# Issuing the last scan of each group behind the first in-projection half of the next group

## What is computed

```
proj = hidden_states @ in_proj_w.T
gate, xBC, dt = split(proj)                      # 8192 gate, 10240 xBC, 128 dt
xBC = silu(causal_conv4(xBC) + conv_b)
x, Bm, Cm = split(xBC)                           # 8 groups of B and C, 128 heads of 64
scores = (C B^T) * exp(segment sums of dt*A)     # per head, causal
Y = scores @ (x*dt) + x*D
yg = Y * silu(gate)
out = yg * rsqrt(mean over the group of yg^2 + eps) * norm_w @ out_proj_w.T
```

## Time and profile before

| | |
|---|---|
| median of 3 runs | 2484.99 us (2480.08 to 2488.39) |
| the profiled execution | 2485.11 us |
| its span, first to last instruction | 2483.3 us |
| mean granted TensorE clock | 0.954 of full |
| PE busy | 2285.2 us, 92% of the span |
| DVE busy | 1697.0 us, 68% |
| ACT busy | 1379.5 us, 56% |
| POOL busy | 846.0 us, 34% |

### The profile page before, as it was taken

The page is one execution under the profiler, slowest core; times in us unless marked ns, Lnnn a source line. Parts: engine busy times, 40 slices in busy tenths (PEclk is TensorE's granted clock), DMA queues, the critical chain, the costliest instruction groups (busy, mean ns, idle before and its releaser), DMA issues. The chain is left out here.

```text
span 2483.3 us, 38330 instructions
## 1 busy us (share of the span) xinstructions
PE 2285.2 (92%) x11624; PEld 1633.1 (66%) x11624; DVE 1697.0 (68%) x2949; ACT 1379.5 (56%) x3105; POOL 846.0 (34%) x681
## 2 busy tenths in 40 slices
PE   6898888897899999999999999999999999987998
PEld 4554545445677776777767777677776777756877
DVE  3555555554797598489579759848957975965345
ACT  4453535403785487388468558737846855852330
POOL 4251423310244244244325414414432541441230
PEclk9699998899999999999999999999999999988999
DMA  5000000001210110111011011011101101002100
GB/s 226 10 1 9 1 1 1 1 0 47 72 34 20 52 31 28 44 31 35 11 60 35 20 52 31 28 48 31 31 24 48 35 20 52 27 1 85 42 18 34
DMA packets 38226, 85.39 MB, mean 34 GB/s; under 512 B 3584, under 2 KB 5888, under 8 KB 37376
## 3 DMA queue, kind: packets, MB, share of 16 engines
q1 hardware_dynamic: 38016, 82.82, 10.1%
HBM read 79.92 MB, written 2.88 MB: 33 GB/s over the span
## 5 line engine op out<-in xcount | busy, mean ns | idle before, releaser
L1643 PE MATMUL b_ps<-xh_keep,wh 128*128 128x512 f32 x1152 | 490.9, 426 | 5.2 <-DVE bc L1398 3.0
L1645 PE MATMUL b_ps<-xh_keep,wl 128*128 128x512 f32 x1152 | 463.1, 402 | 0.0
L1644 PE MATMUL b_ps<-xl_keep,wh 128*128 128x512 f32 x1152 | 463.0, 402 | 0.0
L1434 DVE TENSOR_TENSOR decayed<-decay,b_scores 128x768 f32<-128x768 f32 x256 | 397.8, 1554 | 25.1 <-ACT decay L1162 24.1
L1323 POOL TENSOR_TENSOR wl<-wraw,wh 128x512 fp32r<-128x512 f32 x144 | 190.9, 1326 | 574.7 <-ACT wh L1111 574.7
L1156 ACT ACTIVATE decay<-b_ps,cs 128x256 f32<-128x256 f32 (+1 forms) x1024 | 345.1, 424 | 7.7 <-PE b_ps L1653 7.1
L1398 DVE SCALAR_TENSOR_TENSOR xs<-b_ps,par,xs 128x510 f32<-128x510 f32 (+2 forms) x384 | 284.9, 742 | 93.2 <-ACT xs L1130 80.9
L1643 PEld LDWEIGHTS b_ps<-xh_keep,wh 128*128 128x128 f32 x1152 | 222.0, 193 | 84.2 <-issue 41.5
L1645 PEld LDWEIGHTS b_ps<-xh_keep,wl 128*128 128x128 f32 x1152 | 221.5, 192 | 53.4
L1644 PEld LDWEIGHTS b_ps<-xl_keep,wh 128*128 128x128 f32 x1152 | 223.1, 194 | 42.2
L1524 DVE SCALAR_TENSOR_TENSOR yl<-yg,par,yh 128x512 fp32r<-128x512 f32 x128 | 96.4, 758 | 203.5 <-ACT yh L1177 202.4
(11 more groups left out here) (229 smaller groups left out, 4116.3 us busy)
## 6 DMA issues: line engine op xcount, KB each, us to landing
wraw<-win_dram SPq DMA_DIRECT2D x144, 256.0 KB, 2.6
oraw<-wout_dram SPq DMA_DIRECT2D x8, 2048.0 KB, 9.4
w<-w_dram SPq DMA_DIRECT2D x2, 3584.0 KB, 23.9
fraw<-wgu_dram SPq DMA_DIRECT2D x11, 512.0 KB, 3.5
draw<-wd_dram SPq DMA_DIRECT2D x1, 2816.0 KB, 11.9
xT<-xT_dram SPq DMA_DIRECT2D x4, 512.0 KB, 3.8
x_keep<-x_dram SPq DMA_DIRECT2D x1, 2048.0 KB, 11.2
out_dram<-x_keep SPq DMA_DIRECT2D x8, 256.0 KB, 2.0
```

What stands on the lines that cost most here:

```text
L1434: nc.vector.tensor_tensor(sd[:, b % 2, :, :], ex[:, b % 2, :, :], sm[:, b, :].unsqueeze(1).to_broadcast([P, 2, 3 * P]), ALU.mult)\
L1643: nc.tensor.matmul(out, w_h, x_h, start=(k == 0), stop=False)
L1644: nc.tensor.matmul(out, w_h, x_l, start=False, stop=False)
L1645: last = nc.tensor.matmul(out, w_l, x_h, start=False, stop=(k == KT - 1))
```

## The change

The last scan of a group is no longer issued at the end of `steps`, unless it is the last group. In the loop it is issued after X0_0 of the next group, the first of the four in-projection halves, and ahead of X0_1. Only the order on PE changes. No instruction is added or removed, and the orders of DVE, ACT, POOL and SP stay as they were.

```
@@ in steps(ph, g, last) of the tensor block
                         turn(ph, j + 1, 0)
                         turn(ph, j + 1, 1)
-                scan(ph, UNITS - 1, BATCH - 1)
+                if last:
+                    scan(ph, UNITS - 1, BATCH - 1)
@@ in the loop of the tensor block
                 steps(ph, i, False)
                 for q, c in enumerate(conv_halves(0)):
                     in_half(ph, i, SUBS + 2 + q // 2, c[0])
+                    if q == 0:
+                        scan(ph, UNITS - 1, BATCH - 1)
                 project(ph, i)
                 head_end(ph)
```

## The result

The change made the kernel slower by a third of a percent. The changed kernel takes 2492.72 us (median of 12 runs, 2487.62 to 2498.21), the kernel before 2485.71 us (12 runs, 2480.0 to 2488.39). The ratio is 1.0033, with a 95% interval of 1.0023 to 1.0043. The profiled execution of the changed kernel has a span of 2490.5 us against 2483.3 us, 7.2 us more.

The account below looks back on a forecast made before the run. A chain on DVE, ACT and POOL was taken to bound the stretch from last scan to projection, PE only fitting in. 15.8 us paid, less 1.6 and 1.3, gave +12.8 on 2485.1: 2497.9 us, range 2484 to 2505.

Parts of the forecast that it names:

- PE's wait goes, 19.4 us: Ahead of the last scan in seven loop rounds, PE's wait for DVE's decay product disappears: 7 x 2.77 = 19.4 us.
- The chain holds, and the wait comes back in two parts: DVE, ACT and POOL keep the projection's start at 15.87 us; PE's 2.78 us return as waits of about 2.9 and 2.5.
- Gain in rounds 1 and 7, 1.3 us: From last scan to projection, X0_0 issued sooner brings 16.52 and 16.56 us down to 15.87, 1.3 us gained.
- The clock, 15.8 us paid less 1.6 us: Projection's first two units start at low clock: 7 x 2.25 = 15.8 us paid, less 1.6 that round 3 pays already.
- the two units: Sign: the projection's first two units take 13.3 to 14.6 us, at a granted clock of 0.77 to 0.88.
- Nothing else moves: Elsewhere no change: SP's queue and the DMAs hang on untouched work, and group 7 keeps its order.
- Chain bound, clock kept: Rival at the projection: waits move but the clock rarely falls there; 2483.8 to 2490.6 us; chance 0.20.
- PE bound: Rival: the chain gives way when PE runs ahead, removed wait gained in full, 19.4 us, 2465.7 us; chance 0.07.
- The wait stays: Rival ahead of the last scan: product later than X0_0's end, or X0_0 waits; within 1 us of 2485.1; chance 0.05.
- The wait of line 1734: Sign at the transposes of the sums of squares (line 1733 before): waits for DVE's convolution, 7 x 2.9 = 20 us.
- that of yl: Sign at line 1744 of before: PE's waits for DVE's yl grow from 12.5 us in total to some 24.

## Why the prediction was right, and where it was not

It forecast slower, 2497.9 us in a range of 2484 to 2505; measured were 2492.7 us, or +7.0 us where +12.8 were forecast. The bound of 0.3% that it set for slower was just passed: the ratio is 1.0033, with part of its interval below. That the kernel is slower at all is clear, that it is so by more than 0.3% is not.

*PE's wait goes, 19.4 us.* Right: line 1665 keeps 2.3 us, in group 7.

*The chain holds, and the wait comes back in two parts.* Right. Forecast were 15.87 us, waits of about 2.9 and 2.5 us and PE done 12.15 us after its start; measured 15.88 to 15.89 us from the decay product (15.93 in round 2 before, as 15.87 was counted from the scan), 2.97 and 1.86 to 2.29 us, and 12.3 us in round 2. In four rounds the second wait is 2.29 us, 0.2 less than forecast: the second four transposes begin 12.97 us after the product, not 12.8, and take 0.63 us, not 0.5. In rounds 1, 4 and 7 they take 1.06, 0.77 and 0.76 us, since the low clock has reached them, and the wait is shorter by that. The kernel with matmuls ahead of its scan shows it in all seven rounds, and the one with the scan behind all halves shows where the chain passes.

*Gain in rounds 1 and 7, 1.3 us.* Right; all rounds together gained 1.4 to 1.6.

*The clock, 15.8 us paid less 1.6 us.* Right in mechanism and size. Forecast were +14.2 us for the projection's first two units, measured +14.3 and +14.1. The price per round was 1.9 to 2.9 us above the 11.72 us of the kernel before, with a mean of 2.29; 2.25 was taken. That the two are so near is in part luck: 2.25 was the middle between two ends and not worked out, and the prediction's own mean stretch gave 2.0. The rate behind it held: the low clock covers 34.1 us of these units in the seven rounds, 4.9 us each, and 4.9 x 1.61 / 3.5 is 2.2. It is the clock and not the scan: with the waits filled the two units are at 11.7 us. The Trainium skill, "TensorE: Matmul & The Clock Gate", section "HAM oscillation — how this bites in real kernels", says of a kernel with waits for DMA that the burst of matmuls behind each wait begins cold. The trace of the changed kernel agrees at the projection in all seven rounds (0.79 to 0.85); in the trace of before one wait of 2.8 us in seven left the clock full.

*Nothing else moves.* This is the step that failed, by 5.2 us in the profile, which is most of what lies between +12.8 and +7.2. Two stretches that the change does not touch became shorter, the one ahead of the decay products by 1.4 us and group 7 with what follows by 3.8 us. In group 7 from its first wait in unit 0, to the same place in its last unit (windows, before and then changed):

```profile
2083.86:2201.90 118.04, 115.88 (x648) 82.81 (x649) 105.63 (x124) 96.72 (x206) 49.23 (x35) 0.97 0.07 21
```

```profile
2094.83:2209.97 115.14, 112.99 (x648) 80.99 (x649) 105.39 (x124) 96.49 (x206) 49.22 (x35) 1.00 0.07 22
```

The same matmuls, 2.9 us less: the clock fell in unit 0 of group 7 before and not in the changed kernel. The last 0.9 us of the 3.8 lie behind group 7's last decay product (275.0 us before, 274.1 changed), and no run shows why. Unit 0 of every group has waits of 1.6 and 1.4 us for ACT, behind which the clock falls in some rounds and not in others. Which ones is the same in both profiles of each kernel; my reading is that it hangs on when the waits come, and so on everything ahead of them, which no run isolates. The prediction had priced those low stretches at the same in both kernels. They made 4.3 us of the error: 2.9 in group 7, and 1.4 in the rounds, where both kernels have 30.6 us of them but in different places. The kernel with these waits filled shows what they are worth in all: 16.5 us.

*Rivals.* "Chain bound, clock kept" fails on the granted clock of 0.79 to 0.85 in all seven rounds. "PE bound" fails on the kernel with matmuls ahead of its scan. "The wait stays" fails on the trace. The prediction counted five waits for yl of 0.5 to 1.2 us that left the projection at full clock; the trace of before has six, of 0.49 to 1.31 us, which does not change the argument.

*Signs to look for.* The wait of line 1734 was forecast at 20 us (20.8), that of yl at 24 (19.8), the two units at 13.3 to 14.6 us (13.58 to 14.63). The 24 was also added up too high: the seven waits ahead of the projection were 8.0 us of the 12.5 before, and with 2.5 us each instead they give 22.

## What to carry to other kernels

Before removing a wait of the busiest engine, look at the next thing it waits for, and compare rounds in which it ran at different speeds: if the end comes at the same distance in all of them, another chain sets it, and the removed wait only moves. Then ask what the idle time does in its new place. In this kernel waits of TensorE ahead of the projection, which it sets the pace of, cost 1.9 to 2.9 us a round, since what follows starts at the low clock; the clock's fall behind the 2.8 us wait, ahead of work with slack, had cost 0.7 us in two rounds and nothing in four. And when a chain is shortened, see what its steps will now lie beside: here yl started 1.6 us sooner, took 1.0 us longer beside POOL, and 0.6 us was left.

## What the runs showed of the hardware

- Useless work made a kernel faster: 20 matmuls of 512 columns a round in waits took the changed kernel from 2492.7 us to 2482.8, and 11 in two waits of every group took the kernel before from 2485.2 us to 2468.7. The granted clock is the reason in both, 1.00 (2.4 GHz) instead of stretches at the half level (1.2 GHz).
- The reverse too: 10 useless matmuls that kept the clock full where there was slack made the kernel before 2.3 us slower, as the low stretch came later, where it was paid for.
- Behind the waits of 1.6 and 1.4 us in unit 0 the clock fell in seven of eight groups of the kernel before and in five of eight of the changed one; behind a single one of 2.8 us it fell in six of seven rounds of the kernel before.
- A yl write of 0.74 us took 1.75 us beside a subtraction of POOL, and POOL's took 1.7 us instead of 1.3. It shows as longer busy time on both engines, not as a wait.
- Two executions of the changed kernel needed 1456.2 us for the seven rounds, with the low stretches in the same places, though they began them at 633.7 and 636.5 us. It is not so everywhere: the stretch ahead of the loop, the same instructions in all thirteen profiles, took 628.3 us in one and 636.7 in another, at a granted clock of 0.91 and 0.89. The twelve runs of the kernel before scatter by 8.4 us, and this stretch alone could make nearly all of that.
